# A CIN tower with table look-ups by matrix product: three more fields looked up, the start reordered, the mixed tile in rounded products

## The chip, the cores and the metric

One core of one Trainium2 chip runs the whole kernel. The time is device microseconds of one execution, the median over the runs shown. A profiled execution gives the span (first to last instruction) and every instruction's place in it.

## The reference, cut to what matters

For each of 2048 samples, 39 ids pick one row of 16 floats from each of 39 tables. The tables have 1000 rows (11 fields), 1250 rows (4 fields), 12500 or 125000. A compressed interaction network follows, two layers of products of all fields with all fields, and then a small MLP.

```python
e = jnp.stack([tbl_0[ids[:, 0]], ..., tbl_38[ids[:, 38]]], axis=1)      # [B, 39, 16]
for W in (W0, W1):
    inter = (x[:, :, None, :] * x_emb[:, None, :, :]).reshape(B, last * F, D)
    x = jnp.einsum('bid,hi->bhd', inter, W)                              # 128 outputs
    outs.append(x.sum(axis=-1))
h = jnp.concatenate([z, dense_ctx], axis=1)
h = jnp.maximum(h @ W_top1 + b_top1, 0.0)
h = jnp.maximum(h @ W_top2 + b_top2, 0.0)
y = h @ W_top3
```

## The kernel before, in words

The batch is cut into 16 tiles of 128 samples. A tile is 4 chunks of 32 samples, `g` counts the 64 chunks, `t` the tiles and `c` the chunk within its tile. All five engines run a program written out in full, with semaphores between them; nothing reorders it.

**Rows of a tile.** GpSimd gathers 28 fields a tile with one indirect DMA each (L346) into `e_rows`, which has two buffers. The other 11 fields, all of 1000 rows, are looked up by matrix product in three sets. An id is split into a row of 125 and one of 8 parts. The row numbers of a tile are spread over 125 partitions by a DMA from `id_scratch` (`spread_ids`, L277, into `id_spread`). VectorE compares them with the partition's number (`make_one_hot`, L597), TensorE multiplies with the table (`look_up`, L357), and VectorE masks and sums the 8 parts (`pick_rows`, L611 and L622). For tile t+2 this is done during chunks 1, 2 and 3 of tile t; the third set's `pick_rows` stands in chunk 0 of the tile after. Then `copy_e` (L590) makes a second layout, `e_d`.

**Bases.** SyncE writes `e_rows` to `eT_scratch` (L243) and `e_d` to `e_scratch` (L238), doubles `eT_scratch` in DRAM (L249), and loads from it, for each half tile, five "bases" of 117 x 1024 floats (`load_bases`, L261, 468 KB each). `load_bases(u)` waits until the products of the two chunks that used the buffer are made. The small blocks `e_diag` come per chunk in eight DMAs (`spread`, L270). SyncE issues all of these itself, in one order:

```python
for g in range(CHUNKS):
    t, c = divmod(g, CPT)
    if c == 1 and t + 1 < TILES:
        double_eT(t + 1)
    if g % 2 == 0 and g // 2 + 1 < HALVES:
        load_bases(g // 2 + 1)
    if c == 0 and t + 2 < TILES:
        spread_ids(t + 2)
    spread(g)
```

**A chunk.** Seven products of bases make layer 0, in four groups of 2, 2, 2 and 1. VectorE multiplies (`multiply`, L643), ScalarE rounds to fp32r (`round_products`, L497), VectorE subtracts to get the lower part (`lower_parts`, L651), and TensorE takes three matmuls for each (`contract`, L367, L368, L371). One of the seven, product 3 (`NATIVE`, the mixed tile), skips the rounding and is multiplied in native fp32 (L365). TensorE fills the gaps with layer 1 and the MLP of earlier tiles (`filler`), which end eight chunks after the last one.

**The start.** SyncE loads ids, identity, 11 tables, then all weights (`w1T` alone is 2.5 MB), then stores the row numbers, and spreads them for tile 0; for tile 1 it waits until tile 0's comparisons are done. VectorE looks up tile 0 and tile 1 before `copy_e(0)`.

Of the kernel before, what the change touches and what calls it, by code (L numbers as in the profile page):

```python
# [41 lines left out]
SET_FIRST = tuple(sum(len(p) for q in SETS[:n] for p in q) for n in range(len(SETS) + 1))  # L42
SET_MAX = max(SET_FIRST[n + 1] - SET_FIRST[n] for n in range(len(SETS)))

# [12 lines left out]
LOOK_AT = (1, 2, 3)  # L57
GROUPS = ((0, 1, 2, 0), (0, 3, 2, 2), (1, 2, 2, 4), (2, 3, 1, 6))
NG = len(GROUPS)
NATIVE = 3  # L60
# [39 lines left out]
def cin_tower(nc, dense_t, ids, tables, w_top1, b_top1, w_top2, b_top2, w_top3, w0, w1,  # L100
# [7 lines left out]
    with ctx:  # L108
# [12 lines left out]
        w0_native = sb("w0_native", [R, H])  # L121
# [11 lines left out]
        k_number = sb("k_number", [128, VK])  # L133
        numbers_i = sb("numbers_i", [128, 1 + VK], i32)
        id_row = sb("id_row", [128, TILES, NS])
        id_turned = sb("id_turned", [128, 2, TB], bf16)
        id_spread = sb("id_spread", [VP, NS, TB], bf16)
        id_k = sb("id_k", [128, NS, TILES])
        tab = sb("tab", [VP, NS, VK * D])
        one_hot = [sb(f"one_hot{n}", [VP, SET_MAX, TB]) for n in range(2)]  # L140
        k_mask = sb("k_mask", [128, NS, VK])
        masked = sb("masked", [128, SET_MAX, VK, D])

# [25 lines left out]
        id_part = staging[:, 2 * NT * H + H1:2 * NT * H + H1 + 2 * NS * TILES].bitcast(i32).rearrange("p (a t s) -> p a t s", a=2, s=NS)  # L169
# [25 lines left out]
        id_spread_ready = sem("id_spread_ready")  # L195
# [13 lines left out]
        eT_doubled = sem("eT_doubled")  # L209
        bases_ready = [sem(f"bases_ready{n}") for n in range(2)]  # L210
# [24 lines left out]
        def _(sp):  # L235
# [14 lines left out]

            def load_bases(u):
# [5 lines left out]
                for a, starts in enumerate(BASES):  # L257
                    step = starts[1] - starts[0]
                    half = eT_scratch[t, starts[0]:starts[0] + 1, h * HB:(h + 1) * HB, :].rearrange("f b d -> f (b d)")
                    blocks = bass.AP(half.tensor, half.offset, [[TB * D, F], [step * TB * D, BLOCKS], [1, HALF]])  # L260
                    sp.dma_start(bases[u % 2][:, a, :], blocks).then_inc(bases_ready[u % 2], 16)  # L261
# [30 lines left out]
            for n, f in enumerate(LOOKED):  # L292
                sp.dma_start(tab[:, n, :], tables[f].rearrange("(p k) d -> p (k d)", k=VK)).then_inc(tab_loaded, 16)
            sp.wait_ge(zeroed, 1)
            for n in range(3):
                sp.dma_start(wt1_dense_f[n * GAP:n * GAP + D, :], w_top1[2 * H:2 * H + D, :]).then_inc(wt1_dense_loaded, 16)
            sp.dma_start(w1T[:, :, :], w1).then_inc(w1_loaded, 16)
# [5 lines left out]

            sp.wait_ge(id_turned_ready, 2)
            rows_of_ids = id_scratch.rearrange("t s b -> (t s) b")
            sp.dma_start(rows_of_ids[0:128, :], id_turned[:, 0, :]).then_inc(id_stored, 16)
            sp.dma_start(rows_of_ids[128:TILES * NS, :], id_turned[0:TILES * NS - 128, 1, :]).then_inc(id_stored, 16)
            spread_ids(0)
            spread_ids(1)
            store_e(0)  # L310
            store_eT(0)
            double_eT(0)
# [456 lines left out]
```

## Time and profile before

| | |
|---|---|
| median of 3 runs | 825.3 us (805.21 to 829.03) |
| the profiled execution | 819.52 us |
| its span | 817.7 us |
| TensorE / VectorE / ScalarE / GpSimd busy | 87% / 75% / 48% / 68% |
| granted TensorE clock, mean | 0.989 of full speed |
| DMA | 114.21 MB, mean 140 GB/s |

Busy shares are averages over a start of about 85 us in which no products are made, a steady part of 14 tiles, and an end without gathers. A row of the trace gives start, duration, engine, source line, output<-input, a count where equal instructions are merged, and in brackets how long the engine was idle before it and what ended that. "SPq" rows are SyncE's issuing of DMAs, not the transfers.

### The profile page before, as it was taken

The numbers are of one execution on the slowest core, as the hardware profiler recorded it, in microseconds if no ns is written. First come the engines' busy times: TensorE is split into PE (matmuls) and PEld (weight loads), VectorE is DVE, ScalarE is ACT, GpSimd is POOL, SyncE is SP. The second block draws the span as 40 slices with busy tenths as digits, with TensorE's granted clock in tenths as the row PEclk, the third lists the DMA queues.
The fourth block names the chain that finished last, engine by engine and source line by source line (L and its number), as shares of the span: only waits on it lengthen the run. The fifth ranks groups of instructions, "written<-read, shape, count | busy, mean of one in ns | idle before, by whom it ended". The sixth has DMA issues, their size and how long they took to land.

```text
span 817.7 us, 16181 instructions
## 1 busy us (share of the span) xinstructions
PE 711.4 (87%) x5826; PEld 584.7 (72%) x5826; DVE 610.3 (75%) x790; ACT 393.4 (48%) x769; POOL 552.6 (68%) x454
## 2 busy tenths in 40 slices
PE   0230688989999999999999999999799999999997
PEld 0130465767888787888788878878588878788887
DVE  2260799978796997989797969697698979697710
ACT  0000355545464555556464646464465646465642
POOL 6777888867887788688788778587778888300000
PEclk9999999998999999999999999999899999999999
DMA  7316969586666767686868676677459586654000
GB/s 218 86 24 152 190 156 177 151 160 167 152 135 142 136 162 144 161 168 149 170 146 162 166 158 136 172 140 174 100 126 189 137 162 167 146 160 126 13 7 1
DMA packets 171474, 114.21 MB, mean 140 GB/s; under 512 B 135683, under 2 KB 147939, under 8 KB 171011
## 3 DMA queue, kind: packets, MB, share of 16 engines
q1 hardware_dynamic: 155222, 108.71, 55.3%
q0 software_dynamic: 14336, 3.70, 6.6%
q8 instruction: 46, 0.75, 0.4%
q10 hardware_dynamic: 1837, 0.78, 0.4%
q14 instruction: 33, 0.27, 0.1%
HBM read 102.69 MB, written 15.52 MB: 145 GB/s over the span
## 4 chain that ended last, share of the span: by engine, by line
POOL 67%; issue 19%; PE 12%; DMA 1%; ACT 0%; DVE 0%; POOLq 0%; ACTq 0%; DVEq 0%
POOL e_rows L346 67%; PE z_ps L407 3%; PE x_ps L367 1%; PE x_ps L368 1%; PE g_ps L397 1%; PE x_ps L371 1%; PE x1T_ps L428 1%; DMA e_rows<-in_tbl_dram,ids_sb 1%; PE x_ps L365 1%; PE x1T_ps L420 1%; PE x1T_ps L418 1%; PE x1T_ps L386 0%; PE x1T_ps L437 0%; DVE products L643 0%; DMA ids_sb<-in_ids_dram 0%
## 5 line engine op out<-in xcount | busy, mean ns | idle before, releaser
L346 POOL DMA_INDIRECT e_rows<-in_tbl_dram,ids_sb x448 | 552.1, 1232 | 151.5 <-issue 149.8
L497 ACT CAST product_hi<-products 117x1024 fp32r<-117x1024 f32 (+1 forms) x256 | 214.9, 839 | 205.5 <-DVE products L643 203.6
L643 DVE TENSOR_TENSOR products<-bases 117x1024 f32<-117x1024 f32 (+1 forms) x256 | 277.5, 1084 | 28.6 <-DMA bases<-eT_scratch 25.9
L651 DVE TENSOR_TENSOR product_lo<-products,product_hi 117x1024 fp32r<-117x1024 f32 (+1 forms) x256 | 243.8, 952 | 27.1 <-ACT product_hi L497 27.0
L367 PE MATMUL x_ps<-product_hi,w_hi 117*128 117x512 f32 x384 | 193.9, 505 | 31.8 <-ACT product_hi L497 28.8
L407 PE MATMUL z_ps<-G,w1T 128*128 128x128 f32 x1248 | 178.6, 280 | 0.0
L407 PEld LDWEIGHTS z_ps<-G,w1T 128*128 128x128 f32 x1248 | 165.5, 191 | 16.6 <-issue 0.5
L368 PE MATMUL x_ps<-product_hi,w_lo 117*128 117x512 f32 x384 | 152.2, 396 | 0.0
L371 PE MATMUL x_ps<-product_lo,w_hi 117*128 117x512 f32 x384 | 135.3, 407 | 18.7 <-DVE product_lo L651 16.9
L367 PEld LDWEIGHTS x_ps<-product_hi,w_hi 117*128 117x128 f32 x384 | 73.6, 192 | 59.9 <-issue 48.7
L371 PEld LDWEIGHTS x_ps<-product_lo,w_hi 117*128 117x128 f32 x384 | 72.1, 191 | 45.9 <-DVE product_lo L651 31.1
L518 ACT COPY G<-g_ps 128x320 f32<-128x320 f32 x256 | 102.8, 431 | 0.0
L368 PEld LDWEIGHTS x_ps<-product_hi,w_lo 117*128 117x128 f32 x384 | 73.3, 191 | 22.1 <-issue 15.7
L357 PE MATMUL aux_ps<-tab,one_hot 125*128 125x128 f32 x352 | 53.7, 299 | 39.5 <-DVE one_hot L597 39.5
L397 PEld LDWEIGHTS g_ps<-e_diag,x1T 32*128 32x128 f32 x2048 | 63.3, 186 | 26.7 <-issue 26.6
L357 PEld LDWEIGHTS aux_ps<-tab,one_hot 125*128 125x128 f32 x352 | 48.7, 212 | 41.8 <-issue 24.8
L397 PE MATMUL g_ps<-e_diag,x1T 32*128 32x80 f32 x2048 | 72.7, 278 | 4.2 <-ACT G L518 3.8
L365 PE MATMUL x_ps<-products,w_native 117*128 117x512 f32 x128 | 67.1, 606 | 0.0
L503 ACT COPY x<-x_ps 128x512 f32<-128x512 f32 x64 | 37.3, 583 | 61.7 <-PE x_ps L371 61.6
L590 DVE COPY e_d<-e_rows 128x624 f32<-128x624 f32 x16 | 11.2, 699 | 59.4 <-DMA e_rows<-in_tbl_dram,ids_sb 59.2
L597 DVE TENSOR_SCALAR one_hot<-id_spread,row_number 125x512 f32<-125x512 bf16 (+1 forms) x48 | 23.6, 492 | 39.4 <-DMA id_spread<-id_scratch 38.9
L622 DVE TENSOR_REDUCE e_rows<-masked 128x48 f32<-128x384 f32 (+2 forms) x80 | 47.9, 632 | 1.7
(50 smaller groups left out, 428.8 us busy)
## 6 DMA issues: line engine op xcount, KB each, us to landing
bases<-eT_scratch SPq DMA_DIRECT2D x160, 468.0 KB
e_diag<-e_scratch SPq DMA_DIRECT2D x512, 10.0 KB
e_rows<-in_tbl_dram,ids_sb POOLq DMA_INDIRECT x448
id_spread<-id_scratch SPq DMA_DIRECT2D x16, 343.8 KB
e_scratch<-e_d SPq DMA_DIRECT2D x16, 320.0 KB, 10.5
eT_scratch<-e_rows SPq DMA_DIRECT2D x16, 312.0 KB, 10.2
eT_scratch<-eT_scratch SPq DMA_DIRECT2D x16, 312.0 KB
w1T<-in_L_rec_W_dram SPq DMA_DIRECT2D x1, 2496.0 KB, 10.8
```

The source lines that it names most:

```text
L346: nc.gpsimd.indirect_dma_start(out=e_rows[t % E_SLOTS][:, f * D:(f + 1) * D], out_offset=None, in_=tables[f], in_offset=bass.IndirectOffse ...
L357: last = nc.tensor.matmul(aux_ps[:, m * TB:(m + 1) * TB], one_hot[(t * len(SETS) + n) % 2][:, m, :], tab[:, s, :], start=True, stop=True)
L365: nc.tensor.matmul(x1_ps[:, :], w0_native[:, :], products[:, NATIVE, :], start=False, stop=False)
L367: nc.tensor.matmul(x1_ps[:, :], w0_hi[:, k, :], product_hi[:, k, :], start=(k == 0), stop=False)
L368: nc.tensor.matmul(x1_ps[:, :], w0_lo[:, k, :], product_hi[:, k, :], start=False, stop=False)
L371: last = nc.tensor.matmul(x1_ps[:, :], w0_hi[:, k, :], product_lo[:, k, :], start=False, stop=(k == NT - 1))
L397: last = nc.tensor.matmul(g_ps[r][:, q, :, :], x1T[r * KR:(r + 1) * KR, q, :], e_diag[g % 2][r * KR:(r + 1) * KR, :, q, :], start=True, st ...
L407: last = nc.tensor.matmul(z2_ps[:, :], w1T[:, j, :], G[:, j, t % 2 * TB:(t % 2 + 1) * TB], start=(j == 0), stop=(j == F - 1))
L497: nc.scalar.copy(product_hi[:, first:first + count, :], products[:, first:first + count, :]).then_inc(hi_ready, 1)
L518: nc.scalar.copy(G[:, :, first:first + QB], g_ps[r][:, :, :, :].rearrange("i q n f -> i f (q n)")).then_inc(g_ready, 1)
L643: nc.vector.tensor_tensor(products[:, first:first + count, :], bases[u % 2][:, b:b + count, cols], bases[u % 2][:, a:a + 1, cols].to_broad ...
L651: nc.vector.tensor_tensor(product_lo[:, first:first + count, :], products[:, first:first + count, :], product_hi[:, first:first + count, : ...
```

## The change

- `SETS` gets a fourth set, fields 11, 19 and 27 of 1250 rows (125 rows of 10 parts each). 14 fields are looked up and 25 gathered. The tile's four sets are compared in chunks 0, 1, 2 and 3; the first three are picked in chunks 1, 2, 3 and the fourth in chunk 0 of the next tile. The masks of parts are made in two instructions.
- `id_spread` gets two buffers, each with a semaphore. `spread_ids(t + 2)` stays at its place in SyncE's loop.
- The mixed tile goes through rounding and three matmuls like the others; `w0_native` goes.
- SyncE at the start: row numbers are stored and spread (both tiles) before the weights, the first half tile's bases come in two pieces of 32 samples with a semaphore each, and the weights are loaded only after these. `copy_e(0)` stands before the look-ups of tile 1. ScalarE's wait for the MLP weights moves to chunk 10.

```diff
-SETS = (((0, 5, 10), (1,)), ((14, 24, 34),), ((17, 25), (32, 37)))
+SETS = (((0, 5, 10), (1,)), ((14, 24, 34),), ((17, 25), (32, 37)), ((11, 19, 27),))
+SET_K = (8, 8, 8, 10)
-LOOK_AT = (1, 2, 3)
+LOOK_AT = (0, 1, 2, 3)
...
             def spread_ids(t):
                 sp.wait_ge(id_stored, 32)
-                after(sp, one_hot_ready, t * len(SETS))
-                sp.dma_start(id_spread[:, :, :], id_scratch[t:t + 1, :, :].to_broadcast([VP, NS, TB])).then_inc(id_spread_ready, 16)
+                after(sp, one_hot_ready, (t - 1) * len(SETS))
+                sp.dma_start(id_spread[t % 2][:, :, :], id_scratch[t:t + 1, :, :].to_broadcast([VP, NS, TB])).then_inc(id_spread_ready[t % 2], 16)
...
             spread_ids(0)
             spread_ids(1)
-            store_e(0)
             store_eT(0)
+            store_e(0)
             double_eT(0)
-            load_bases(0)
+            sp.wait_ge(eT_doubled, 16)
+            for c in range(2):
+                load_base_part(0, c * (HB // 2), HB // 2, first_ready[c])
+
+            sp.dma_start(w1T[:, :, :], w1).then_inc(w1_loaded, 16)
...
             def contract(g, n):
-                if NATIVE in range(GROUPS[n][3], GROUPS[n][3] + GROUPS[n][2]):
-                    nc.tensor.matmul(x1_ps[:, :], w0_native[:, :], products[:, NATIVE, :], start=False, stop=False)
-                for k in in_parts(n):
+                for k in range(first, first + count):
...
             def make_one_hot(t, n):
                 if n == 0:
-                    dve.wait_ge(id_spread_ready, (t + 1) * 16)
+                    dve.wait_ge(id_spread_ready[t % 2], (t // 2 + 1) * 16)
...
+            copy_e(0)
             make_k_mask(1)
             for n in range(len(SETS)):
                 make_one_hot(1, n)
                 pick_rows(1, n)
-            copy_e(0)
             multiply(0, 0)
...
-                if c == 2 and t + 2 < TILES:
-                    pick_rows(t + 2, 0)
-                if c == 3 and t + 2 < TILES:
-                    pick_rows(t + 2, 1)
+                if c > 0 and t + 2 < TILES:
+                    pick_rows(t + 2, c - 1)
                 if c == 0 and 1 <= t and t + 1 < TILES:
-                    pick_rows(t + 1, 2)
+                    pick_rows(t + 1, 3)
```

VectorE at the turn of a tile, before. `products` of 512 is the last group of a chunk, and the 1024-wide ones are groups 0 to 2; the rows run from the last product of one tile's chunk 3 to the `copy_e` in the next tile's chunk 0.

```order
L643 TENSOR_TENSOR products<-bases 117x512
L651 TENSOR_TENSOR product_lo<-products,product_hi 117x1024
L643 TENSOR_TENSOR products<-bases 117x1024
L651 TENSOR_TENSOR product_lo<-products,product_hi 117x512
L643 TENSOR_TENSOR products<-bases 117x1024
L651 TENSOR_TENSOR product_lo<-products,product_hi 117x1024
L643 TENSOR_TENSOR products<-bases 117x1024
L651 TENSOR_TENSOR product_lo<-products,product_hi 117x512
L611 TENSOR_TENSOR masked<-aux_ps,k_mask 128x512
L622 TENSOR_REDUCE e_rows<-masked 128x2x16 x2
L590 COPY e_d<-e_rows 128x16x39
```

The same place in the changed kernel.

```order
L654 TENSOR_TENSOR products<-bases 117x512
L662 TENSOR_TENSOR product_lo<-products,product_hi 117x1024
L654 TENSOR_TENSOR products<-bases 117x1024
L662 TENSOR_TENSOR product_lo<-products,product_hi 117x512
L654 TENSOR_TENSOR products<-bases 117x1024
L662 TENSOR_TENSOR product_lo<-products,product_hi 117x1024
L605 TENSOR_SCALAR one_hot<-id_spread,row_number 125x512
L654 TENSOR_TENSOR products<-bases 117x1024
L662 TENSOR_TENSOR product_lo<-products,product_hi 117x1024
L622 TENSOR_TENSOR masked<-aux_ps,k_mask 128x480
L632 TENSOR_REDUCE e_rows<-masked 128x3x16
L598 COPY e_d<-e_rows 128x16x39
```

A comparison (`one_hot`) for the tile two further now stands five instructions behind the last product of the old tile; before, the first one stood in chunk 1.

SyncE in the first chunks, from the spreading of the first row numbers on, before.

```order
L277 DMA id_spread<-id_scratch 125x1408 x2
L238 DMA e_scratch<-e_d 128x640
L243 DMA eT_scratch<-e_rows 128x39x16
L249 DMA eT_scratch<-eT_scratch 16x4992
L261 DMA bases<-eT_scratch 117x1x1024 x10
L277 DMA id_spread<-id_scratch 125x1408
L270 DMA e_diag<-e_scratch 16x4x40 x8
```

The same in the changed kernel.

```order
L281 DMA id_spread<-id_scratch 125x1792 x2
L242 DMA eT_scratch<-e_rows 128x39x16
L237 DMA e_scratch<-e_d 128x640
L248 DMA eT_scratch<-eT_scratch 16x4992
L257 DMA bases<-eT_scratch 117x1x512 x10
L314 DMA w1T<-in_L_rec_W_dram 128x4992
L315 DMA wt_cin<-in_W_top_dram 128x2x512
L316 DMA wt<-in_W_top_dram 128x4x256
L317 DMA wt<-in_W_top_dram 128x2
L318 DMA bias<-in_b_top_dram 128x4
L257 DMA bases<-eT_scratch 117x1x1024 x5
L281 DMA id_spread<-id_scratch 125x1792
```

The weights, which stood ahead of everything here, now stand between the first half tile's bases and the second's; the row numbers of tile 2 still follow the second half's bases, as in every later tile.

## Rows read from the trace of the kernel before

**Rows 1.** Page, part 4: the chain that ended last, by engine

```profile
POOL 67%; issue 19%; PE 12%; DMA 1%; ACT 0%; DVE 0%; POOLq 0%; ACTq 0%; DVEq 0%
```

**Rows 2.** Groups by line and shape: xcount | busy us, mean ns | idle before

```profile
L346 POOL DMA_INDIRECT e_rows<-in_tbl_dram,ids_sb x448 | 552.1, 1232 | 151.5 <-issue 149.8 <-DMA ids_sb<-in_ids_dram 1.8
...
L357 PE MATMUL aux_ps<-tab,one_hot 125*128 125x128 f32 x352 | 53.7, 299 | 39.5 <-DVE one_hot L597 39.5
...
L622 DVE TENSOR_REDUCE e_rows<-masked 128x48 f32<-128x384 f32 x32 | 26.1, 815 | 1.1
...
L611 DVE TENSOR_TENSOR masked<-aux_ps,k_mask 128x384 f32<-128x384 f32 x16 | 8.8, 549 | 3.5 <-PE aux_ps L357 3.5
L597 DVE TENSOR_SCALAR one_hot<-id_spread,row_number 125x384 f32<-125x384 bf16 x16 | 7.1, 444 | 0.0
```

**Rows 3.** Timeline of VectorE, one tile: start us, duration us

```profile
397.55 0.72 DVE L590 COPY e_d<-e_rows 128x624 f32<-128x624 f32 x1 [5.66 <-DMA e_rows<-in_tbl_dram,ids_sb]
...
427.15 1.23 DVE L651 TENSOR_TENSOR product_lo<-products,product_hi 117x1024 fp32r<-117x1024 f32 x1 [0.61 <-ACT product_hi L497]
...
429.43 0.68 DVE L651 TENSOR_TENSOR product_lo<-products,product_hi 117x512 fp32r<-117x512 f32 x1
430.03 1.22 DVE L643 TENSOR_TENSOR products<-bases 117x1024 f32<-117x1024 f32 x1
431.17 1.22 DVE L651 TENSOR_TENSOR product_lo<-products,product_hi 117x1024 fp32r<-117x1024 f32 x1
432.30 1.22 DVE L643 TENSOR_TENSOR products<-bases 117x1024 f32<-117x1024 f32 x1
...
440.11 0.69 DVE L590 COPY e_d<-e_rows 128x624 f32<-128x624 f32 x1 [4.27 <-DMA e_rows<-in_tbl_dram,ids_sb]
```

**Rows 4.** Timeline of SyncE's queue: bases issued in chunk 0 of two tiles

```profile
430.47 4.61 SPq L261 DMA_DIRECT2D bases<-eT_scratch  x5
...
473.59 5.04 SPq L261 DMA_DIRECT2D bases<-eT_scratch  x5
```

**Rows 5.** Timeline: one spreading of row numbers, and who waited for it

```profile
300.01 4.34 SPq L261 DMA_DIRECT2D bases<-eT_scratch  x5
304.46 0.70 SPq L277 DMA_DIRECT2D id_spread<-id_scratch  x1
...
317.32 0.49 DVE L597 TENSOR_SCALAR one_hot<-id_spread,row_number 125x512 f32<-125x512 bf16 x1 [3.90 <-DMA id_spread<-id_scratch]
```

**Rows 6.** Timeline of VectorE, the end: last `copy_e`, and two waits four chunks apart

```profile
711.00 0.71 DVE L590 COPY e_d<-e_rows 128x624 f32<-128x624 f32 x1 [6.61 <-DMA e_rows<-in_tbl_dram,ids_sb]
...
738.98 1.23 DVE L651 TENSOR_TENSOR product_lo<-products,product_hi 117x1024 fp32r<-117x1024 f32 x1 [1.75 <-ACT product_hi L497]
...
779.33 1.86 DVE L651 TENSOR_TENSOR product_lo<-products,product_hi 117x1024 fp32r<-117x1024 f32 x2 [1.75 <-ACT product_hi L497]
```

**Rows 7.** Timeline of SyncE's queue, the start

```profile
26.88 13.87 SPq L277 DMA_DIRECT2D id_spread<-id_scratch  x2
...
62.10 0.39 SPq L243 DMA_DIRECT2D eT_scratch<-e_rows  x1
...
71.05 4.51 SPq L261 DMA_DIRECT2D bases<-eT_scratch  x5
```

**Rows 8.** Timeline of VectorE, the start; L681 follows tile 0's look-ups

```profile
31.82 0.49 DVE L597 TENSOR_SCALAR one_hot<-id_spread,row_number 125x512 f32<-125x512 bf16 x1 [23.00 <-DMA id_spread<-id_scratch]
...
44.27 1.08 DVE L681 TENSOR_TENSOR G<-G 117x896 f32<-117x896 f32 x1
...
98.74 0.49 DVE L597 TENSOR_SCALAR one_hot<-id_spread,row_number 125x512 f32<-125x512 bf16 x1 [1.42 <-DMA id_spread<-id_scratch]
```

**Rows 9.** DMA issues: KB each, us from issue to landing

```profile
bases<-eT_scratch SPq DMA_DIRECT2D x160, 468.0 KB
...
id_spread<-id_scratch SPq DMA_DIRECT2D x16, 343.8 KB
...
w1T<-in_L_rec_W_dram SPq DMA_DIRECT2D x1, 2496.0 KB, 10.8
```

More of the change, by code:

```diff
@@ L42 @@
 SET_FIRST = tuple(sum(len(p) for q in SETS[:n] for p in q) for n in range(len(SETS) + 1))
+K_OF = tuple(SET_K[n] for n, parts in enumerate(SETS) for part in parts for f in part)
+K_FIRST = tuple(sum(K_OF[:n]) for n in range(NS + 1))
+EIGHTS, TENS = SET_FIRST[3], NS - SET_FIRST[3]
 SET_MAX = max(SET_FIRST[n + 1] - SET_FIRST[n] for n in range(len(SETS)))
@@ L132, in cin_tower @@
         row_number = sb("row_number", [128, 1])
-        k_number = sb("k_number", [128, VK])
-        numbers_i = sb("numbers_i", [128, 1 + VK], i32)
+        k_number = sb("k_number", [128, MAX_K])
+        numbers_i = sb("numbers_i", [128, 1 + MAX_K], i32)
         id_row = sb("id_row", [128, TILES, NS])
         id_turned = sb("id_turned", [128, 2, TB], bf16)
-        id_spread = sb("id_spread", [VP, NS, TB], bf16)
-        id_k = sb("id_k", [128, NS, TILES])
-        tab = sb("tab", [VP, NS, VK * D])
+        id_spread = [sb(f"id_spread{n}", [VP, NS, TB], bf16) for n in range(2)]
+        id_k = sb("id_k", [128, TILES, NS])
+        tab = sb("tab", [VP, K_FIRST[NS] * D])
         one_hot = [sb(f"one_hot{n}", [VP, SET_MAX, TB]) for n in range(2)]
-        k_mask = sb("k_mask", [128, NS, VK])
-        masked = sb("masked", [128, SET_MAX, VK, D])
+        k_mask = sb("k_mask", [128, K_FIRST[NS]])
+        masked = sb("masked", [128, COLS])
         ids_sb = sb("ids_sb", [128, TILES, F], i32)
@@ L194, in cin_tower @@
         id_stored = sem("id_stored")
-        id_spread_ready = sem("id_spread_ready")
+        id_spread_ready = [sem(f"id_spread_ready{n}") for n in range(2)]
         one_hot_ready = sem("one_hot_ready")
@@ L209, in cin_tower @@
         eT_doubled = sem("eT_doubled")
+        first_ready = [sem(f"first_ready{n}") for n in range(2)]
         bases_ready = [sem(f"bases_ready{n}") for n in range(2)]
@@ L249, in double_eT, with load_base_part @@
                 sp.dma_start(eT_scratch[t, F:2 * F, :, :], eT_scratch[t, 0:F, :, :]).then_inc(eT_doubled, 16)
+            def load_base_part(t, first, count, ready):
+                at = first % HB * D
+                for a, starts in enumerate(BASES):
+                    step = starts[1] - starts[0]
+                    part = eT_scratch[t, starts[0]:starts[0] + 1, first:first + count, :].rearrange("f b d -> f (b d)")
+                    blocks = bass.AP(part.tensor, part.offset, [[TB * D, F], [step * TB * D, BLOCKS], [1, count * D]])
+                    sp.dma_start(bases[first // HB][:, a, at:at + count * D], blocks).then_inc(ready, 16)
             def load_bases(u):
@@ L256, in load_bases @@
                 after(sp, product_ready, (u - 1) * 2 * NG)
[L257 to L261, printed above, removed]
+                load_base_part(t, h * HB, HB, bases_ready[h])
             def spread(g):
@@ L369, in contract @@
                 pe.wait_ge(lo_ready, g * NG + n + 1)
-                for k in in_parts(n):
+                for k in range(first, first + count):
                     last = nc.tensor.matmul(x1_ps[:, :], w0_hi[:, k, :], product_lo[:, k, :], start=False, stop=(k == NT - 1))
@@ L493, in round_products @@
             def round_products(g, n):
[L494 removed]
+                _, _, count, first = GROUPS[n]
                 act.wait_ge(product_ready, g * NG + n + 1)
@@ L638, in multiply @@
                 cols = slice(g % 2 * COLS, (g % 2 + 1) * COLS)
-                dve.wait_ge(bases_ready[u % 2], (u // 2 + 1) * 16 * LOADS)
+                if u == 0:
+                    dve.wait_ge(first_ready[g], 16 * LOADS)
+                else:
+                    dve.wait_ge(bases_ready[u % 2], (u // 2 + u % 2) * 16 * LOADS)
                 after(dve, lo_ready, (g - 1) * NG + n + 1)
-                if NATIVE in range(first, first + count):
-                    after(dve, contracted, (g - 1) * NG + n + 1)
                 nc.vector.tensor_tensor(products[:, first:first + count, :], bases[u % 2][:, b:b + count, cols],
@@ L647, in lower_parts @@
             def lower_parts(g, n):
-                first, count = in_parts(n)[0], len(in_parts(n))
+                _, _, count, first = GROUPS[n]
                 dve.wait_ge(hi_ready, g * NG + n + 1)
@@ L718, in _ @@
                 lower_parts(g, 2)
-                if c == 1 and t + 2 < TILES:
+                if c == 0 and t + 2 < TILES:
                     make_k_mask(t + 2)
```

91 lines of the change are left out of this document (51 added, 40 removed).

## The prediction

> **What bounds the kernel now.** I read the chain that ended last first: 67% of it is GpSimd [rows 1], the gathers. The groups then give their price: 448 gathers busy 552.1 us, idle 151.5 us between them [rows 2], so 703.6 / 448 = 1.57 us each and 28 x 1.57 = 44.0 us a tile. VectorE's timeline shows the period: `copy_e` at 397.55 and at 440.11, 42.6 us, and from 397.55 to 711.00 seven tiles, 44.8 us each [rows 3, 6]. In the tile shown VectorE stands still for 4.27 us waiting for gathers and 0.61 us elsewhere [rows 3], so its own work is 42.56 - 4.88 = 37.7 us a tile. The end, without gathers or look-ups, shows the third one: VectorE then waits once a chunk for ScalarE, which waits for TensorE, and four chunks take 779.33 - 738.98 = 40.4 us [rows 6]. The look-up matmuls are 53.7 us in all [rows 2], at most 3.4 us a tile, so TensorE wants up to 43.8. GpSimd, TensorE and SyncE's own order are all near 44, VectorE at 38. Taking work off one of them is worth little; a wait on VectorE longer than its 5 to 6 us of slack is worth its full excess.
>
> The decisive reading is what the row numbers (`id_spread`) wait for. SyncE issues five bases at 300.01 and the row numbers at 304.46, and the comparison that waits for them starts at 317.32 [rows 5]: 17.3 us after the first of the bases, 12.9 after their own issue. Six comparisons in the loop ended such a wait; counted from the bases' first issue five of them took 16.1 to 17.7 us, mean 16.9 (the sixth, at 98.74, had ten bases ahead). At the start, with no bases ahead, the same transfer took 31.82 - 26.88 = 4.9 us [rows 7, 8]. So the numbers come behind 5 x 468 KB [rows 9].
>
> **Fewer gathers.** 25 x 1.57 = 39.3 us a tile on GpSimd, 4.7 less. That removes VectorE's wait at `copy_e` and nothing else, since what follows is later than this.
>
> **VectorE's added work.** Slots are the distances between starts: 1.14 us for 1024 columns (430.03 to 431.17) and 0.60 for 512 (429.43 to 430.03) [rows 3]. The mixed product's lower part makes one 512 instruction a 1024 one in each chunk, 4 x 0.54 = 2.2 us a tile. The comparison of three more fields is 0.44 less an overlap of some 0.06, 0.4. Its masking is wider than the 384 of the 0.55 us row, 480 columns, some 0.65; its sum is 0.82 x 480 / 384 = 1.0 less the overlap, 0.95 [rows 2]. A second mask instruction is 0.1 to 0.2. Sum 4.3, and VectorE's work is 42.0 us a tile. For 480 columns no row stands; between no longer than 384 and twice that, the error is under 1.5 us a tile.
>
> **TensorE's.** Two native passes and one weight go for three rounded matmuls: near zero either way, between -0.5 and +0.5 us a tile, I take 0. Three fields with 160 columns add 6 of 28 matmuls, a quarter longer: at most 53.7 / 16 x (6 x 1.25 / 22) = 1.1 us [rows 2]. TensorE wants 45 us at most, and the period below hides it. ScalarE's rounding grows by 4 x 0.4 us and is hidden by half an idle engine.
>
> **The comparison in chunk 0.** This is the large term. The first comparison for tile t+2 moves from chunk 1 to chunk 0. SyncE issues the row numbers where it did, behind five bases, and it may issue these only when the last product of tile t-1 is made (call it P). On VectorE only five instructions stand between P and the comparison: from 427.15 less its wait of 0.61, 426.54, to 432.30 less nothing, with that 0.61 taken out, 5.2 us [rows 3]. The second buffer frees an order that did not bind: the condition is met a tile earlier, both with it and without. So:
>
> - from P to the bases' first issue: 0.3 us if SyncE stands ready. SyncE's row after `copy_e` says when it can: 473.59 - 440.11 = 33.5 us later [rows 3, 4]. In the changed kernel P comes 36.8 (below) after the comparison, `copy_e` 4.5 after it (0.4 + 1.14 + 1.14 + 0.65 + 0.95 and gaps), so SyncE would be ready at 38.0, 1.2 late. But SyncE's own instructions there stretch while the transfers in front are not through, and here the queue is empty at `copy_e`. I take 0.3, the bounds are 0 and 1.2.
> - from there to the landing: 16.9, plus the numbers' growth from 343.8 KB by 3/11, 94 KB. 2340 KB of bases and 344 KB took 16.9, so 94 more take 0.4 to 0.6: 17.4. Bounds 16 and 18.5, from the rows' own spread.
> - VectorE stands for 0.3 + 17.4 - 5.2 = 12.5 us, in each of 14 tiles (t = 0 to 13).
>
> Queued behind the waiting comparison are products 2 and 3 of chunk 0, the picks of tile t+1 and `copy_e(t+1)`; TensorE, with at most a chunk in hand, runs dry. After it VectorE has 42.0 - 5.2 = 36.8 us to the next P. Period: 0.3 + 17.4 + 36.8 = 54.5 us, against 44.8. TensorE's 45 and GpSimd's 39 fit inside.
>
> The Trainium skill says in "DMA: Bandwidth & Descriptors", section "Queues, rings and completion order", that descriptors on one DMA engine are consumed in ring order, but that completion is not first in, first out per issuing engine. If that let the small transfer finish ahead, the first rival below would hold; the 12.9 us of [rows 5] against 4.9 us of [rows 7, 8] speak for the whole wait.
>
> **The start.** Row numbers no longer stand behind the weights. They are stored at about 13 us and spread at 17, so land at 17 + 4.9 = 22. Three sets took 44.27 - 31.82 = 12.5 [rows 8], four take 16.7: `e_rows` of tile 0 is whole at 39. Storing and doubling took 71.05 - 62.10 = 9.0 [rows 7]: 48, when the bases are issued; products start at about 61, after tile 1's look-ups, not at 85.6. But the first comparison for tile 2 now stands in chunk 0 and behind everything: the first half's bases (14.5 us, 71.05 to 85.6, in pieces of half the size), the weights (w1T's 2496 KB in 10.8 us [rows 9], a megabyte more, say 13 together), the second half's bases and the numbers (another 14.5). 48 + 14.5 + 13 + 14.5 = 90. So the comparison starts at 90 (84 to 98), with chunk 0 half done. Before, it stood at 98.74 with one chunk more done, 8.5 us: the start gains nothing that lasts. The 25 us won are spent waiting here.
>
> **Sum.** Comparison of t=0 at 90. Of t=13 at 90 + 13 x 54.5 = 798.5. From there 36.8 to P, 5.2, two instructions of 1.14 and the picks 1.6: `copy_e(15)` at 844.4. From the last `copy_e` to the end it was 817.7 - 711.0 = 106.7, bound by TensorE, and stays so. Span 951; the profiled execution has 1.8 us outside its span (819.5 to 817.7): 953. I take off 3 for bases that land quicker with fewer gathers beside them: 950 us, 1.16 of the profiled execution, which is 0.7% under the median of the runs shown.
>
> **Rivals.**
> - *The row numbers don't wait for the bases.* Then they come at the bases' issue, 4.6 us [rows 4], 0.5 of their own, 4.9 and 0.5 for size: 10.5 after the first. Stall 5.6, period 47.6, end 90 lower by up to 7: 950 - 13 x 6.9 - 5 = 855 us. For it: at a start the transfer is this quick. Against: all five waits of 16 us and more. Still slower than before.
> - *Faster: the numbers land within VectorE's 5.2 us, and the gathers were the bound.* VectorE has 42.0, GpSimd 39.3, TensorE up to 45: about 44.0 a tile against 44.8, and the start gives some 15 us before chunk 2's bases come behind the weights. 819.5 - 11 - 15 = 794 us. It decides as soon as landing less than 5.2 us after P is possible; issuing five bases alone takes 4.6 [rows 4]. The case holds if the numbers are fetched a tile ahead, which the written order excludes.
> - *SyncE is late.* If its instructions keep their length, P to issue is 1.2 us and more, and lengthens with wider numbers; 2 us late make 950 + 13 x 1.7 = 972 us. Nothing excludes it, since before it went through its list nearly without a pause.
> - *The new instructions leave the work as it was:* VectorE's slack absorbs the stall. It has 5 to 6 us, the gathers' wait, and this is in the sum already.
>
> **How the numbers follow.** Mechanism and sizes as summed: 0.72. SyncE late: 0.17. Numbers early: 0.06. Faster: 0.03; within 2%, by a mixture of early numbers and a better start: 0.02. Runs of before scatter by 3%, so 2% is about what can be told from no change. Stalls of 10.5 to 14 us a tile give 950 -26/+20, the start -6/+8, so the range is 908 to 988. Faster 0.03, same 0.02, slower 0.95.
>
> **What would show it.** The comparison of 512 in chunk 0 has 10 to 14 us idle before it, ended by the DMA of `id_spread`, 14 times, 150 to 190 us in all; `copy_e` has no more waits for gathers; GpSimd is idle between tiles with a wait for `e_d`; `copy_e` comes every 54 us; the first product at about 61 us and the first such comparison near 90. A period under 48 would make the queueing wrong. If the waits are there but the period is over 56, SyncE is late. If bases and not numbers end the waits, the sum is right by accident.

## The result, and the profile after

The changed kernel takes 957.13 us (median of 4 runs, 953.52 to 960.79), against 820.78 us for the kernel before over its four runs by then. The ratio is 1.181, 95% interval 1.164 to 1.197; here and in every experiment it leaves out executions that ran over 1.5% longer than the fastest of the same kernel (of before 825.3 and 829.03), so it is not the quotient of the two medians. The forecast was 950 us, in a range of 908 to 988.

The page of the changed kernel, parts 1 and 4, beside [rows 1]:

```profile
span 959.0 us, 16576 instructions
...
PE 743.2 (78%) x5986; PEld 631.6 (66%) x5986; DVE 674.2 (70%) x860; ACT 421.8 (44%) x769; POOL 517.2 (54%) x406
...
PE 34%; DVE 23%; DMA 22%; SPq 14%; issue 6%; ACT 1%; DVEq 1%; ACTq 0%
DMA id_spread<-id_scratch 20%; DVE product_lo L662 9%; DVE products L654 8%; SPq L257 7%; PE z_ps L414 6%; PE x_ps L378 5%; PE x_ps L374 4%; PE x_ps L375 4%; PE g_ps L404 4%; SPq L274 4%; PE aux_ps L364 3%; DVE e_rows L632 3%; PE x1T_ps L435 2%; DVE masked L622 2%; PE x1T_ps L427 2%
```

GpSimd, which was 67% of the chain that ended last, is gone from it. In its place stands the transfer of the row numbers with 20%, the issuing of the bases in front of it (SPq L257), and VectorE.

Its waits, in total, with the number of times and the longest:

```profile
DVE one_hot L605 <- DMA id_spread<-id_scratch: 214.0, 15, 28.8
...
POOL e_rows L352 <- DMA eT_scratch<-e_rows: 161.8, 12, 15.4
PE x_ps L378 <- DVE product_lo L662: 155.2, 27, 28.2
```

The first line is the cause. The other two are consequences: GpSimd has finished its 25 gathers and waits for a free buffer (until `e_rows` is stored), and TensorE has run out of lower parts. There is no line for `copy_e` waiting for gathers any more, which had 59 us before.

One turn of a tile, VectorE and SyncE in the timeline of the changed kernel, beside [rows 3] and [rows 5]:

```profile
181.07 0.69 DVE L654 TENSOR_TENSOR products<-bases 117x512 f32<-117x512 f32 x1
...
181.83 4.61 SPq L257 DMA_DIRECT2D bases<-eT_scratch  x5
...
185.67 1.23 DVE L662 TENSOR_TENSOR product_lo<-products,product_hi 117x1024 fp32r<-117x1024 f32 x1
...
186.55 0.78 SPq L281 DMA_DIRECT2D id_spread<-id_scratch  x1
...
199.33 0.49 DVE L605 TENSOR_SCALAR one_hot<-id_spread,row_number 125x512 f32<-125x512 bf16 x1 [12.43 <-DMA id_spread<-id_scratch]
...
203.75 0.69 DVE L598 COPY e_d<-e_rows 128x624 f32<-128x624 f32 x1
```

The old tile's last product ends at 181.7. SyncE stood ready and issues the bases at once. VectorE does its five instructions to 186.9, and the comparison starts at 199.33, 17.5 us after the first of the bases. The first, second and last of the fourteen such waits in the loop:

```profile
93.86 0.49 DVE L605 TENSOR_SCALAR one_hot<-id_spread,row_number 125x512 f32<-125x512 bf16 x1 [28.81 <-DMA id_spread<-id_scratch]
145.87 0.48 DVE L605 TENSOR_SCALAR one_hot<-id_spread,row_number 125x512 f32<-125x512 bf16 x1 [12.73 <-DMA id_spread<-id_scratch]
...
804.17 0.49 DVE L605 TENSOR_SCALAR one_hot<-id_spread,row_number 125x512 f32<-125x512 bf16 x1 [14.14 <-DMA id_spread<-id_scratch]
```

The period is (804.17 - 93.86) / 13 = 54.6 us. Thirteen of the waits are 12.35 to 14.14 us, mean 13.15. With the first they make 199.8 of the 214.0 us above; the remaining 14.2 are the wait for tile 0's numbers at the very start.

### The profile page after: what moved, and what is told of

Read it like the earlier page. It is cut to its first block, busy times and chain, and to the rows that moved or that the text cites. A ratio compares the mean times of both kernels' runs of the same rounds, so it can differ in the third digit from the quotient of the medians.

```text
span 959.0 us, 16576 instructions
## 1 busy us (share of the span) xinstructions
PE 743.2 (78%) x5986; PEld 631.6 (66%) x5986; DVE 674.2 (70%) x860; ACT 421.8 (44%) x769; POOL 517.2 (54%) x406
## 3 DMA queue, kind: packets, MB, share of 16 engines
q1 hardware_dynamic: 156310, 110.49, 44.8%
## 4 chain that ended last, share of the span: by engine, by line
PE 34%; DVE 23%; DMA 22%; SPq 14%; issue 6%; ACT 1%; DVEq 1%; ACTq 0%
DMA id_spread<-id_scratch 20%; DVE product_lo L662 9%; DVE products L654 8%; SPq L257 7%; PE z_ps L414 6%; PE x_ps L378 5%; PE x_ps L374 4%; PE x_ps L375 4%; PE g_ps L404 4%; SPq L274 4%; PE aux_ps L364 3%; DVE e_rows L632 3%; PE x1T_ps L435 2%; DVE masked L622 2%; PE x1T_ps L427 2%
## 5 line engine op out<-in xcount | busy, mean ns | idle before, releaser
L352 POOL DMA_INDIRECT e_rows<-in_tbl_dram,ids_sb x400 | 516.8, 1292 | 281.7 <-DMA eT_scratch<-e_rows 161.8
L504 ACT CAST product_hi<-products 117x1024 fp32r<-117x1024 f32 (+1 forms) x256 | 242.2, 946 | 357.6 <-DVE products L654 356.4
L662 DVE TENSOR_TENSOR product_lo<-products,product_hi 117x1024 fp32r<-117x1024 f32 (+1 forms) x256 | 277.9, 1086 | 11.9 <-ACT product_hi L504 11.9
L378 PE MATMUL x_ps<-product_lo,w_hi 117*128 117x512 f32 x448 | 159.4, 427 | 158.2 <-DVE product_lo L662 155.2
L414 PEld LDWEIGHTS z_ps<-G,w1T 128*128 128x128 f32 x1248 | 178.4, 205 | 18.7 <-issue 0.4
L375 PE MATMUL x_ps<-product_hi,w_lo 117*128 117x512 f32 x448 | 181.9, 406 | 0.0
L605 DVE TENSOR_SCALAR one_hot<-id_spread,row_number 125x512 f32<-125x512 bf16 x64 | 29.3, 458 | 214.0 <-DMA id_spread<-id_scratch 214.0
L364 PE MATMUL aux_ps<-tab,one_hot 125*128 125x128 f32 (+1 forms) x448 | 71.4, 305 | 35.3 <-DVE one_hot L605 35.3
L375 PEld LDWEIGHTS x_ps<-product_hi,w_lo 117*128 117x128 f32 x448 | 88.7, 198 | 10.4
L632 DVE TENSOR_REDUCE e_rows<-masked 128x48 f32<-128x384 f32 (+1 forms) x96 | 64.0, 694 | 2.2
L622 DVE TENSOR_TENSOR masked<-aux_ps,k_mask 128x512 f32<-128x512 f32 x64 | 41.2, 644 | 16.3 <-PE aux_ps L364 16.3
L516 ACT COPY x1T<-x1T_ps 128x512 f32<-128x512 f32 x64 | 37.9, 592 | 2.4 <-PE x1T_ps L393 2.4
## 6 DMA issues: line engine op xcount, KB each, us to landing
id_spread<-id_scratch SPq DMA_DIRECT2D x16, 437.5 KB
```

The costliest lines, as they stand in the source:

```text
L352: nc.gpsimd.indirect_dma_start(out=e_rows[t % E_SLOTS][:, f * D:(f + 1) * D], out_offset=None, in_=tables[f], in_offset=bass.IndirectOffse ...
L364: last = nc.tensor.matmul(aux_ps[:, m * width:(m + 1) * width], one_hot[(t * len(SETS) + n) % 2][:, m, :], tab[:, K_FIRST[s] * D:K_FIRST[s ...
L375: nc.tensor.matmul(x1_ps[:, :], w0_lo[:, k, :], product_hi[:, k, :], start=False, stop=False)
L378: last = nc.tensor.matmul(x1_ps[:, :], w0_hi[:, k, :], product_lo[:, k, :], start=False, stop=(k == NT - 1))
L414: last = nc.tensor.matmul(z2_ps[:, :], w1T[:, j, :], G[:, j, t % 2 * TB:(t % 2 + 1) * TB], start=(j == 0), stop=(j == F - 1))
L504: nc.scalar.copy(product_hi[:, first:first + count, :], products[:, first:first + count, :]).then_inc(hi_ready, 1)
```

## The experiments

Each ran with the kernel before on the same chip: 1 to 4 on one chip, 5 to 8 on a second, 9 to 11 on a third. The kernel before scatters by some 3% between executions, while those that fetch the numbers early (below) repeat within 0.1 to 1%. So small differences are read between experiments, and where these ran on different chips, from their traces.

**1. The numbers fetched early.** The changed kernel, with the row numbers of tile t+3 issued in chunk 2 of tile t.

```diff
             double_eT(0)
+            spread_ids(2)
...
-                if c == 0 and t + 2 < TILES:
-                    spread_ids(t + 2)
+                if c == 2 and t + 3 < TILES:
+                    spread_ids(t + 3)
```

> The changed kernel with the row numbers of tile t+3 fetched in chunk 2 of tile t (and those of tile 2 ahead of the first bases), nothing else changed. Theory (the comparison in chunk 0 waits behind five bases): the 14 waits of 12.4 to 14.1 us and the one of 28.8 go, the period falls from 54.6 to 44-46 us (TensorE or SyncE next), time 795-825 us. Rival (the added VectorE and TensorE work makes the kernel slow): 900 us or more. Rival (the fallen TensorE clock, 0.93, is a cause of its own): the clock stays near 0.93 and the period above 47.

Measured 789.76 us (789.37 to 790.45, 4 runs), ratio to before 0.971 (0.960 to 0.982), below the 795 to 825 expected. The waits are gone, and 167 us with them. The added work is all still there. Its chain, and two of its `copy_e`:

```profile
PE 81%; SPq 6%; DMA 6%; DVE 5%; issue 2%; ACT 0%; DVEq 0%; ACTq 0%
```

```profile
462.87 0.83 DVE L599 COPY e_d<-e_rows 128x624 f32<-128x624 f32 x1
506.03 0.83 DVE L599 COPY e_d<-e_rows 128x624 f32<-128x624 f32 x1
```

43.16 us a tile. From 200 to 678 us TensorE is busy for all of the 478 us, at a granted clock of 1.00: this is TensorE's whole work with 28 look-up matmuls. Both rivals of this run fall. This kernel beats both the one before and the changed one.

**2. The numbers ahead of the bases, in the same chunk.**

```diff
+                if c == 0 and t + 2 < TILES:
+                    spread_ids(t + 2)
                 if g % 2 == 0 and g // 2 + 1 < HALVES:
                     load_bases(g // 2 + 1)
-                if c == 0 and t + 2 < TILES:
-                    spread_ids(t + 2)
```

> The changed kernel with the row numbers issued in the same chunk 0, but ahead of the bases instead of behind them. Theory: they land about 5 us after their issue; a wait of 0 to 5 us a tile is left when SyncE gets there late, and the one in tile 0 (behind the weights) stays about 15-20 us. Period 45-49 us, time 820-870 us. Rival (what matters is that they are fetched in the same chunk, not the bases ahead of them): 930 us or more.

Measured 813.81 us (808.48 to 820.87), ratio 0.999 (0.992 to 1.006), better than the 820 to 870 expected. One turn:

```profile
382.14 0.27 SPq L281 DMA_DIRECT2D id_spread<-id_scratch  x1
382.52 5.25 SPq L257 DMA_DIRECT2D bases<-eT_scratch  x5
388.80 0.49 DVE L605 TENSOR_SCALAR one_hot<-id_spread,row_number 125x512 f32<-125x512 bf16 x1 [2.40 <-DMA id_spread<-id_scratch]
```

The numbers land 6.7 us after their issue here, 5.7 to 7.1 in the thirteen tiles behind tile 0. Waits of 0.3 to 4.0 us are left, mean 2.3, and most of that fits into the slack that VectorE (54.6 - 13.15 = 41.5 us of work a tile) has against TensorE's 43.16, which I had not subtracted. The wait of 19.33 us in tile 0, behind the weights, stays as expected. Swapping two calls is worth 143 us.

**3. The kernel before, with its comparisons one chunk earlier.** 28 gathers, 11 fields, native mixed product and the old start stay.

```diff
-LOOK_AT = (1, 2, 3)
+LOOK_AT = (0, 1, 2)
...
-                if c == 2 and t + 2 < TILES:
-                    pick_rows(t + 2, 0)
-                if c == 3 and t + 2 < TILES:
-                    pick_rows(t + 2, 1)
-                if c == 0 and 1 <= t and t + 1 < TILES:
-                    pick_rows(t + 1, 2)
+                if c > 0 and t + 2 < TILES:
+                    pick_rows(t + 2, c - 1)
```

(The masks are made a chunk earlier too.)

> The kernel before (28 gathers, 11 fields, native mixed product, old start) with the comparisons in chunks 0, 1, 2 instead of 1, 2, 3 and the picks one chunk earlier; the row numbers are issued where they were. Theory: VectorE's 37.7 us of work a tile plus 12 us of wait, period about 50 us, time 880-910 us, with 14 waits for the row numbers of 11-13 us each. Rival (the added work is what costs): 815-835 us as before.

Measured 926.0 us (922.58 to 927.64), ratio 1.138 (1.125 to 1.152). The mechanism is as expected, the size above it: after 8.4 us in tile 0 the waits are 11.0 to 14.2 us, and from tile 1 on the period is 51.9.

```profile
387.30 4.48 SPq L261 DMA_DIRECT2D bases<-eT_scratch  x5
391.88 0.54 SPq L277 DMA_DIRECT2D id_spread<-id_scratch  x1
...
404.52 0.65 DVE L597 TENSOR_SCALAR one_hot<-id_spread,row_number 125x512 f32<-125x512 bf16 x1 [12.93 <-DMA id_spread<-id_scratch]
```

SyncE comes late here: it issues the first base 0.8 to 3.0 us after the last product of the old tile, mean 1.9, where in the changed kernel it is 0.5. Three quarters of the change's loss (0.138 of 0.181) come with this one move and none of its added work.

**10. The same with the numbers early.** Experiment 3 with two `id_spread` buffers and the numbers fetched in chunk 2 of the tile before, as in experiment 1.

```diff
-        id_spread = sb("id_spread", [VP, NS, TB], bf16)
+        id_spread = [sb(f"id_spread{n}", [VP, NS, TB], bf16) for n in range(2)]
...
-                if c == 0 and t + 2 < TILES:
-                    spread_ids(t + 2)
+                if c == 2 and t + 3 < TILES:
+                    spread_ids(t + 3)
```

> e3_before_chunk0 (the kernel before with the comparisons in chunks 0, 1, 2) with two id buffers and the row numbers fetched in chunk 2 of the tile before. Theory: its 12 to 14 us of wait a tile go, and it is back at the time of before: 810-832 us, bound by the gathers again. Rival (moving the comparisons and picks a chunk earlier costs something itself): 850 us or more.

Measured 834.54 us (829.85 to 838.24), ratio 1.023 (1.012 to 1.034). The edit takes 91 us back from experiment 3. It ends 2% above the kernel before, just over the 810 to 832 expected: `copy_e` waits for gathers again, and a tile takes 45.9 us.

```profile
492.48 0.71 DVE L591 COPY e_d<-e_rows 128x624 f32<-128x624 f32 x1 [7.16 <-DMA e_rows<-in_tbl_dram,ids_sb]
```

That is 28 gathers at 1.64 us each between 215 and 700 us, against 1.60 before over the same stretch. Why they come at a slightly wider pitch stays open.

**8. The numbers behind two of the five bases.**

```diff
-                load_base_part(t, h * HB, HB, bases_ready[h])
+                load_base_part(t, h * HB, HB, bases_ready[h], t + 2 if h == 1 and t + 2 < TILES else None)
...
                 for a, starts in enumerate(BASES):
+                    if a == 2 and ids is not None:
+                        spread_ids(ids)
...
-                if c == 0 and t + 2 < TILES:
-                    spread_ids(t + 2)
```

> The changed kernel with the row numbers issued behind two of the five bases instead of all five. Theory (the wait is the transfer time of what is issued ahead, about 2.7 us for each of the bases): they land 3 x 2.7 = 8 us sooner, wait about 5 us a tile instead of 13, period 46-47 us, 840-860 us. Rival (the bases of the whole half tile share the engines, whatever the order of issue): wait 9 us or more, 890 us or more.

Measured 906.9 us (905.2 to 908.9), ratio 1.101 (1.089 to 1.112). The rival held:

```profile
376.43 1.68 SPq L259 DMA_DIRECT2D bases<-eT_scratch  x2
378.21 0.41 SPq L283 DMA_DIRECT2D id_spread<-id_scratch  x1
...
388.57 0.49 DVE L605 TENSOR_SCALAR one_hot<-id_spread,row_number 125x512 f32<-125x512 bf16 x1 [7.54 <-DMA id_spread<-id_scratch]
```

10.4 us after their own issue, and this is the quickest tile: over the thirteen behind tile 0 it is 10.4 to 13.4, mean 12.1, where a plain sum over what was issued ahead would have given about 8. That is only 1.0 us less than with all five ahead (mean 13.1 in the changed kernel); the rest of what is won comes from the earlier issue. Waits are 7.5 to 10.5 us. The three bases that are issued behind the numbers delay them too.

**4. The numbers on another queue.** ScalarE issues them on its own queue at the start of chunk 0.

```diff
+                if c == 0 and t + 2 < TILES:
+                    act.wait_ge(id_stored, 32)
+                    after(act, one_hot_ready, (t + 1) * len(SETS))
+                    act.dma_start(id_spread[t % 2][:, :, :], id_scratch[t + 2:t + 3, :, :].to_broadcast([VP, NS, TB])).then_inc(id_spread_ready[t % 2], 16)
```

> The changed kernel with the row numbers of tile t+2 issued by ScalarE on its own DMA queue at the start of chunk 0 (about 3.5 us behind the last product of the old tile), while SyncE issues the bases as before. Theory (the numbers wait in SyncE's queue behind the bases): they share the engines with the bases and land 6 to 10 us after their issue; wait 4 to 8 us a tile, period 46-50 us, 830-880 us. Rival (the DMA engines as a whole are full, the queue does not matter): they land with the bases, wait 12 us or more, 940 us or more.

Measured 954.21 us (953.15 to 955.29), ratio 1.172 (1.159 to 1.186). The rival was right: a queue of its own gave nothing.

```profile
392.38 4.37 SPq L257 DMA_DIRECT2D bases<-eT_scratch  x5
395.88 0.26 ACTq L561 DMA_DIRECT2D id_spread<-id_scratch  x1
...
410.95 0.48 DVE L607 TENSOR_SCALAR one_hot<-id_spread,row_number 125x512 f32<-125x512 bf16 x1 [14.04 <-DMA id_spread<-id_scratch]
```

15.1 us after the issue; over the thirteen tiles behind tile 0 it is 13.3 to 15.8, mean 14.4. The DMA view of the same kernel from 395 to 400 us, right behind the issue (queue, packets, MB, share of the 16 DMA engines):

```profile
q1 hardware_dynamic: 295, 1.09, 77.3%
q0 software_dynamic: 49, 0.01, 12.1%
```

Only SyncE's queue q1 and the gathers move. ScalarE's q10 has no packet yet, 4.1 us behind its issue. From 400 to 403, and from 406 to 410.5, when the bases are thinning out:

```profile
q1 hardware_dynamic: 197, 0.51, 73.8%
q10 hardware_dynamic: 22, 0.08, 11.4%
```

```profile
q1 hardware_dynamic: 374, 0.22, 17.6%
q10 hardware_dynamic: 78, 0.26, 15.3%
```

**11. That queue alone.** Experiment 4, and SyncE holds chunk 0's bases back until the numbers have landed.

```diff
+                if c == 0 and t + 2 < TILES:
+                    sp.wait_ge(id_spread_ready[t % 2], ((t + 2) // 2 + 1) * 16)
                 if g % 2 == 0 and g // 2 + 1 < HALVES:
                     load_bases(g // 2 + 1)
```

> e4_ids_act_queue with SyncE holding the bases of chunk 0 back until the row numbers have landed, so that they travel alone on ScalarE's queue. Theory (in e4 they share the DMA engines with the bases): landing about 6.5 us after their issue instead of 15, as on SyncE's queue with nothing ahead, the comparison waits 4 to 6 us, period 45-48 us, 820-870 us. Rival (a transfer on ScalarE's queue is slow in itself): wait 12 us or more, 940 us or more.

Measured 850.82 us (846.54 to 856.08), ratio 1.043 (1.032 to 1.055).

```profile
403.44 0.26 ACTq L563 DMA_DIRECT2D id_spread<-id_scratch  x1
408.42 1.68 SPq L257 DMA_DIRECT2D bases<-eT_scratch  x2
408.43 0.49 DVE L609 TENSOR_SCALAR one_hot<-id_spread,row_number 125x512 f32<-125x512 bf16 x1 [3.95 <-DMA id_spread<-id_scratch]
```

5.0 us (4.8 to 5.4 in the thirteen tiles), on the same queue that took 15.1 with the bases under way. The first packets of q10 come within 1 us of the issue. From 405 to 408 us, where the numbers travel with only gathers beside them:

```profile
q10 hardware_dynamic: 109, 0.38, 31.4%
```

So even alone this transfer keeps less than a third of the time of the 16 DMA engines busy, while the bases of experiment 4 above took 77%. Whether numbers laid out in another shape would use more of the engines and land sooner was not tried.

ScalarE's queue is not slow in itself, and experiments 4, 8 and 11 together say that the numbers wait for what the bases occupy beyond SyncE's queue, which points to the DMA engines. They do not separate the engines from anything else that both queues may share.

**5 to 7. What the parts are worth once the numbers come early.** Experiment 5 is experiment 1 with the mixed product back in native fp32; 6 is experiment 1 with the weights, `e_d` and `copy_e(0)` in the order of before; 7 is both, so of the change only the three fields are left. The core of 5, against experiment 1 (the fourth K tile then has no rounded and no lower part):

```diff
+                if NATIVE in range(GROUPS[n][3], GROUPS[n][3] + GROUPS[n][2]):
+                    nc.tensor.matmul(x1_ps[:, :], w0_native[:, :], products[:, NATIVE, :], start=False, stop=False)
-                for k in range(first, first + count):
+                for k in in_parts(n):
```

And of 6 (the loads of the weights are the six issues that begin with `w1T`):

```diff
+            sp.dma_start(w1T[:, :, :], w1).then_inc(w1_loaded, 16)
...
             sp.wait_ge(id_turned_ready, 2)
...
-            store_eT(0)
             store_e(0)
+            store_eT(0)
...
-            sp.dma_start(w1T[:, :, :], w1).then_inc(w1_loaded, 16)
...
-            copy_e(0)
             make_k_mask(1)
...
                 pick_rows(1, n)
+            copy_e(0)
```

> e1_ids_early with the mixed product back in native fp32 (no rounding, no lower part, two native passes). e1 is bound by TensorE, 43.15 us a tile at full clock. Theory: the rounded form costs VectorE 2.2 us a tile that is hidden, and saves TensorE about 0.1 us a chunk: native 43.4-43.6 us a tile, 792-800 us. Rival (VectorE's work counts in e1 as well): 2 us less a tile, 760-775 us.

> e1_ids_early with the start in the order of before (weights ahead of the row numbers, the e_d copy and its store first, behind tile 1's look-ups); the two-piece first bases and the row numbers of tile 2 ahead of them stay. Theory: first products at about 85 instead of 61 us, but without the second half's bases behind the weights; the steady part is unchanged. 12 to 18 us slower than e1: 802-808 us. Rival (the new start is worth nothing, as summed for the changed kernel): 788-792 us.

> Native mixed product and the start of before together, so of the change only the three looked-up fields with two id buffers are left, and the row numbers are fetched early. Theory: 43.5 us a tile bound by TensorE against 44.8 before, start as before: 805-815 us, 1 to 3% faster than before. Rival (the gathers were not what bound the kernel before): 820-830 us.

Measured: 5, 800.84 us (798.3 to 804.01), ratio 0.971 (0.961 to 0.981); 6, 813.36 us (813.06 to 815.05), ratio 0.988 (0.977 to 0.998); 7, 821.54 us (817.28 to 823.03), ratio 1.001 (0.997 to 1.005).

Two `copy_e` of experiment 5 give 43.76 us a tile, and so do two of experiment 7:

```profile
428.57 0.81 DVE L608 COPY e_d<-e_rows 128x624 f32<-128x624 f32 x1
472.33 0.82 DVE L608 COPY e_d<-e_rows 128x624 f32<-128x624 f32 x1
```

```profile
403.43 0.81 DVE L608 COPY e_d<-e_rows 128x624 f32<-128x624 f32 x1
447.19 0.70 DVE L608 COPY e_d<-e_rows 128x624 f32<-128x624 f32 x1
```

The rounded mixed product is 0.6 us a tile cheaper for TensorE, some 10 us over sixteen tiles; the two medians differ by 11. Both lie just outside what was expected (43.4 to 43.6 us a tile, 792 to 800 us). Its 2.2 us a tile more on VectorE cost nothing.

The new start is worth 813.36 - 789.76 = 23.6 us, above the 12 to 18 expected, and far from nothing. The traces agree: the last `copy_e` comes at 702.01 instead of 678.25. With the old start the first products come only here:

```profile
94.48 2.36 DVE L655 TENSOR_TENSOR products<-bases 117x1024 f32<-117x1024 f32 x2 [20.43 <-DMA bases<-eT_scratch]
```

The three fields alone are worth nothing in time (7 against before), against an expected 1 to 3%, and 821.54 us lies in the range of the rival (820 to 830), by which the gathers were no bound. The trace speaks against the rival, since the gathers did hold up the kernel before. No `copy_e` waits for gathers any more, TensorE is busy from 228 to 709 us without a gap, and the fourteen tiles between the copies for tile 1 and tile 15 take 609.1 us instead of 620.2. But the copy for tile 1 comes at 100.24 us instead of 90.85, and from the last copy to the end it is 111.5 us instead of 106.7, which together give back 14 us. What makes the start and the end longer was not separated.

**9. The weights still later.** Experiment 1 with the weights issued in chunk 2 of the first tile, behind its bases.

```diff
-            sp.dma_start(w1T[:, :, :], w1).then_inc(w1_loaded, 16)
...
                 spread(g)
+                if g == 2:
+                    sp.dma_start(w1T[:, :, :], w1).then_inc(w1_loaded, 16)
...
```

> e1_ids_early with the weights loaded in chunk 2 of the first tile, behind its bases, instead of between the two halves' bases. e1 waits 1.00 and 4.15 us for bases in the first two tiles and 7.1 us for tile 1's gathers. Theory (the weights in front delay the bases): those two waits go, 3 to 6 us less, 784-787 us. Rival (TensorE, bound from there on, or the gathers set the start): no change, 788-791 us.

Measured 795.21 us (793.37 to 796.32), ratio 0.975 (0.966 to 0.983): 5 us slower than experiment 1, a miss. The traces show the same 5 us (the fifth `copy_e` at 209.32 against 204.31) and then the same 43.15 us a tile.

```profile
132.43 1.23 DVE L656 TENSOR_TENSOR products<-bases 117x1024 f32<-117x1024 f32 x1 [5.41 <-DMA bases<-eT_scratch]
156.09 1.23 DVE L656 TENSOR_TENSOR products<-bases 117x1024 f32<-117x1024 f32 x1 [3.68 <-DMA bases<-eT_scratch]
```

The weights now travel in front of tile 1's second half and tile 2's bases. The wait has moved, and with a longer one.

## Why the prediction was right

**The bound before.** GpSimd, TensorE and SyncE near 44 us a tile, VectorE at 38. Experiment 7 bears out GpSimd and TensorE: three gathers fewer brought 0.8 us a tile, since TensorE's 43.8 is next. (The 44.8 us of the prediction is the mean of seven tiles; that of all fourteen is 44.3.) I had TensorE at 45 at most with the added look-ups; experiment 1 puts it at 43.2. No run gives SyncE a figure of its own; it keeps up with 43.2 in experiment 1.

**The comparison in chunk 0.** P (the end of the old tile's last product) to issue 0.3 was 0.1 in the tile shown, 0.1 to 0.9 over the thirteen, mean 0.5. Issue to landing 17.4 was 17.5 in the tile shown, 17.0 to 18.7, mean 17.8, and VectorE's stretch in between 5.2 was 5.1. The wait of 12.5 was 12.4 to 14.1, mean 13.15. The period of 54.5 was 54.6: the longer wait met somewhat less work than the 42.0 us, 41.5. That these two misses cancel in the period is luck, though only 0.5 us of it. Experiments 1, 2, 3 and 10 show the cause from both sides: fetching early removes 167 us from the changed kernel. In the one before, the comparison in chunk 0 costs 91 us against the same kernel with early numbers, and some 110 us (a ratio of 1.138) against the kernel as it was.

**The reason given for the 17.4 us** was half of it. I wrote that the numbers "come behind 5 x 468 KB", as in one queue. The duration was read from rows and so was right, but the account would have forecast a cure by ScalarE's queue, and experiment 4 shows none. The prediction's reading of 12.9 against 4.9 us spoke for the load of the engines as much as for the queue.

The Trainium skill has the missing half in "DMA: Bandwidth & Descriptors", section "Issuing engines are not separate DMA queues": the transfers of all issuing engines run on the same sixteen DMA engines. Experiment 4 agrees, with 15.1 us against 5.0 in experiment 11. What the Trainium skill says on the same page, in section "Queues, rings and completion order", of turns taken packet by packet between queues is not what the first 4 us behind the issue in experiment 4 look like, in which q10 moved nothing; why it starts so late stays open.

**The start.** First products at 61 were at 61.46. The comparison at 90 was at 93.86, 4 us late. The first bases were issued at 49.17 instead of 48. And the sum gave the second half's bases and the numbers 14.5 us together, which is the price of the bases alone; its own reading for both is 17.4. These two make the 4 us. "The start gains nothing that lasts" was right for the changed kernel only, because the comparison in chunk 0 spent the gain. Experiment 6 shows 23.6 us once that is mended.

**The end.** From the last `copy_e` (849.70) to the end 109.3 us, where 106.7 were carried over.

**The rivals.** "Numbers early" and "faster" need a landing within 5 to 11 us; no tile has one. "SyncE is late" fell as a large term, but not to nothing: the mean of 0.5 us from P to the issue lies inside the bounds of 0 and 1.2. As I had argued from the empty queue, its instructions there were short: issuing the store of `e_d` takes 3.2 us in the loop of the changed kernel, where it takes 7 to 10 in most tiles of the one before. The 3 us taken off for fewer gathers beside the bases were not there.

The 7 us between 950 and 957 are thus the 4 us at the start, 2.6 at the end, those 3, and 13 x 0.1 for the period, which make 11, less the difference of 4 between the profiled execution (960.79) and the median.

**The signs.** Two did not come as written. The fourteen waits are 200 us in all and not 150 to 190, and one is 28.8 and not 10 to 14: that list priced the comparison of the first tile like the others, though the part on the start had it wait for what was won there. And GpSimd waits between tiles for the store of `e_rows`, not for `e_d`.

## What to carry to other kernels

When a consumer is moved forward in a hand-written order, look where its producer is issued, and count the distance between the two, not whether the semaphore's condition is met: the second buffer was there, and the fetch was not moved. A small transfer that is needed soon belongs ahead of the large ones, a tile early if a buffer allows; another queue did not help here while the large ones were under way. And a gather count that tops the chain of waits is worth only its distance to the next engine.

## What the runs showed of the hardware

**The TensorE clock falls in a kernel that waits.** The granted clock was 0.989 before and 0.938 here. By stretches of one tile (columns: TensorE, weight load, VectorE, ScalarE and GpSimd busy, granted clock, DMA share, GB/s):

```profile
181.80:186.90 5.10, 5.10 (x57) 4.41 (x56) 5.10 (x5) 3.90 (x7) 4.49 (x3) 1.00 0.60 142
186.90:199.30 12.40, 5.33 (x47) 4.46 (x40) 0.00 (x0) 0.43 (x1) 9.32 (x10) 0.86 0.72 188
199.30:236.00 36.70, 32.34 (x268) 28.02 (x269) 36.38 (x47) 21.56 (x41) 21.45 (x17) 0.91 0.45 104
```

In the 12.4 us of VectorE's wait TensorE works for 5.3 and then stands, and the mean granted clock falls to 0.86, then 0.91 in the stretch behind, while the first lower-part pair after the wait takes 1.22 us:

```profile
202.14 1.22 PE L378 MATMUL x_ps<-product_lo,w_hi 117*128 117x512 f32 x2 [9.90 <-DVE product_lo L662]
206.61 0.62 PE L378 MATMUL x_ps<-product_lo,w_hi 117*128 117x512 f32 x2
```

Twice the later pair's 0.62, so at 1.2 instead of 2.4 GHz. It cost little here: in that last stretch VectorE is busy for 36.38 of 36.70 us, so the slower TensorE does not hold it up. The kernels whose numbers come early and that TensorE bounds (experiments 1, 5, 6, 7 and 9) have the clock at 1.00 in their steady part.

**Landing of the same 437.5 KB by what surrounds it.** From its own issue to the start of the comparison that waits for it, range and mean of the thirteen tiles behind tile 0:

| | us | mean |
|---|---|---|
| alone on ScalarE's queue (experiment 11) | 4.8 to 5.4 | 5.0 |
| first, five bases behind it (2) | 5.7 to 7.1 | 6.3 |
| two bases ahead, three behind (8) | 10.4 to 13.4 | 12.1 |
| five bases ahead (the changed kernel) | 12.3 to 14.3 | 13.1 |
| on ScalarE's queue, five under way (4) | 13.3 to 15.8 | 14.4 |

The order of issue matters, and so does what is issued afterwards: being second to two bases costs nearly as much as being second to five.
